# Expert stages' routing: router products within the norm, ranks by 16 wide products, one-hot tables in two operations, block experts behind them

## The reference, cut to what matters

```python
def _L0_ffn_ref(x):                       # 1024 tokens of 256, 2 experts, top 1
    probs = softmax(x @ gate_w.T); sel = argmax(probs)
    h = silu(x @ w_gate[e]) * (x @ w_up[e]); y = h @ w_down[e]
    return y[sel] * probs[sel]
def _L1_ffn_ref(x):                       # 8 experts, top 2
    probs = softmax(gelu(x @ rw1) @ rw2); wgt, idx = top_k(probs, 2)
    Ye = gelu(x @ w1[e] + b1[e]) @ w2[e] + b2[e]
    Ce = gelu(b1[e]) @ w2[e] + b2[e]      # for tokens that did not pick e
    return sum over e, k of active * wgt[k] * where(idx[k] == e, Ye, Ce)
x = x + 0.5 * L0_ffn(layernorm(x))
x = x + L0_attn(layernorm(x))
x = x + 0.5 * L0_ffn(layernorm(x))
x = x + 0.5 * L1_ffn(layernorm(x))
x = x + L1_attn(layernorm(x))             # a state-space mixer
x = x + 0.5 * L1_ffn(layernorm(x))
```

## Time and profile before

| | us |
|---|---|
| median of 3 runs | 1038.74 (1035.82 to 1044.8) |
| the profiled execution | 1029.2 |
| its span, first to last instruction | 1027.6 |
| PE busy | 860.1 (84%) |
| DVE, POOL, ACT busy | 595.2, 494.0, 396.2 |
| mean granted clock of PE | 0.939 |

### The profile page before, as it was taken

How to read it: one execution, slowest core, us unless ns; L and a number is a source line. 1 busy time by engine, 2 the same in 40 slices (tenths; PEclk the granted TensorE clock), 3 DMA queues, 4 the chain that set the end, 5 groups by cost and what they waited for, 6 DMA issues and landing times.

```text
span 1027.6 us, 21524 instructions
## 1 busy us (share of the span) xinstructions
PE 860.1 (84%) x7796; PEld 553.8 (54%) x7797; DVE 595.2 (58%) x1107; ACT 396.2 (39%) x955; POOL 494.0 (48%) x536
## 2 busy tenths in 40 slices
PE   3089986778778878999899999868789878999995
PEld 2046642323322334665589999433334444799994
DVE  5623346659888252334655565646589846556555
ACT  6322223127546442223245445356301224444441
POOL 2326758418888531212255453313688832555530
PEclk9999998989989989998799999889999998999997
DMA  8312655445555316202376664230000002666644
GB/s 295 111 39 91 204 181 158 168 179 182 179 180 160 109 46 277 110 16 73 107 249 222 246 228 146 93 138 1 0 1 0 1 6 103 230 245 232 234 160 139
DMA packets 47817, 142.25 MB, mean 138 GB/s; under 512 B 10641, under 2 KB 23778, under 8 KB 41218
## 3 DMA queue, kind: packets, MB, share of 16 engines
q0 software_dynamic: 19280, 93.40, 26.9%
q1 hardware_dynamic: 22430, 40.92, 11.3%
q10 hardware_dynamic: 6036, 6.95, 2.0%
HBM read 106.11 MB, written 35.16 MB: 137 GB/s over the span
## 4 chain that ended last, share of the span: by engine, by line
PE 64%; DVE 14%; DMA 8%; ACT 6%; issue 5%; SPq 2%; POOL 1%; ACTq 0%; DVEq 0%; POOLq 0%
PE psum L570 17%; PE psum L543 12%; PE psum L529 9%; PE psum L1831 4%; PE psum L1324 3%; PE psum L114 2%; DMA wq_dram<-mem 2%; PE psum L554 2%; DMA max_dram<-mem 2%; DVE mem L1454 2%; PE psum L1858 2%; PE psum L516 1%; PE psum L1296 1%; DVE mem L315 1%; PE psum L1272 1%
## 5 line engine op out<-in xcount | busy, mean ns | idle before, releaser
L570 PE MATMUL psum<-mem 128*128 x1536 | 178.9, 273 | 3.6 <-DVE mem L810 2.4
L570 PEld LDWEIGHTS psum<-mem 128*128 128x128 f16 x1536 | 146.3, 98 | 24.0 <-issue 4.8
L919 POOL DMA_INDIRECT y_dram<-mem x64 | 63.6, 993 | 155.2 <-DVE mem L826 153.3
L543 PE MATMUL psum<-mem 128*128 128x128 f16 x2208 | 130.8, 219 | 0.0
L543 PEld LDWEIGHTS psum<-mem 128*128 128x128 f16 x2208 | 126.8, 98 | 0.7
L661 ACT ACTIVATE mem<-psum,mem 128x128 f32<-128x128 f32 x368 | 105.0, 369 | 52.7 <-PE psum L543 51.2
L914 POOL DMA_INDIRECT mem<-xn_dram,mem x64 | 66.8, 1044 | 106.1 <-PE psum L516 79.0
L1408 ACT ACTIVATE mem<-psum 128x512 f32<-128x512 f32 (+1 forms) x160 | 79.9, 552 | 81.9 <-PE psum L1304 53.4
L114 PE MATMUL psum<-ones 128*128 128x512 f16 x324 | 102.5, 441 | 0.6 <-issue 0.6
L529 PE MATMUL psum<-mem 128*128 x432 | 99.7, 389 | 1.6 <-issue 1.6
L1454 DVE TENSOR_REDUCE mem<-psum 128x2 f32<-128x1024 f32 (+2 forms) x96 | 87.9, 948 | 22.3 <-PE psum L1278 12.7
(11 more groups left out here) (250 smaller groups left out, 1477.0 us busy)
## 6 DMA issues: line engine op xcount, KB each, us to landing
stage<-in_w POOLq DMA_DIRECT2D x20, 480.0 KB, 4.9
stage<-in_w POOLq DMA_DIRECT2D x16, 512.0 KB, 4.3
w_rows<-mem SPq DMA_DIRECT2D x8, 1024.0 KB, 7.6
w2h_dram<-mem POOLq DMA_DIRECT2D x20, 240.0 KB, 2.9
w2l_dram<-mem POOLq DMA_DIRECT2D x20, 240.0 KB, 3.4
xn_dram<-mem ACTq DMA_DIRECT2D x32, 128.0 KB, 1.7
mem<-w2h_dram SPq DMA_DIRECT2D x2, 2048.0 KB, 12.7
mem<-w2l_dram SPq DMA_DIRECT2D x2, 2048.0 KB, 17.9
```

Source lines behind the costliest of these rows:

```text
L543: ins = eng.matmul(c.bank(2 * p + j // half)[:, j % half * P:(j % half + 1) * P], mats[q][:, l, k, j * P:(j + 1) * P], x[:, p, k, :], star ...
L570: ins = eng.matmul(c.bank(6)[:, 0:D], a[:, 0 if gated else p, q * half + j, :], w[:, at], start=(i == 0), stop=(i == 3 * CF - 1))
L919: eng.indirect_dma_start(c.y_dram[:, :], bass.IndirectOffsetOnAxis(ap=yidx[:, b:b + 1], axis=0), yo[:, b % 2, :], None).then_inc(s_ys[b % ...
```

## The change

- `layernorm_stage` takes a function `between`, which PE calls for each tile behind its transposes, and a `table`, an activation function that ACT runs once on one element ahead of the norm. Gated: the router products of tiles 0 to 5 are issued in the norm (0, 1 and 2 with tile 4), those of tiles 6 and 7 behind it. Otherwise: the six products of half 0 are issued two by two with tiles 5, 6 and 7, each pair in place of two of the three idle products. The idle products in the norm behind attention write to bank 4 instead of 5.
- ACT runs one more element of Silu or Gelu behind the Exp (not in stage 1).
- Ranks: one product per choice of `before16` with the masks of all tiles (64 columns, 16 gated), then for each tile u and choice one product of `ones16` with u's masks, repeated for all tiles behind it. All accumulate in one region. 16 products instead of 72 (8 instead of 36 gated).
- `ends`, `ebc`, `ebf`, `widx`, `ebi` stand behind the one-hot tables in DVE's order. `ebc` compares with 7 (1) experts instead of 8 (2); two operations disappear (the product by P with the minimum, and a minimum).
- `pcol`, `sbase16`, `eqb` and the counting rows `iota16` are fp16, the latter copied from fp32 at the start of the program. The 16 (8) one-hot tables are made by two two-tensor operations of 8 (4) tables each.
- POOL makes `idb` first, then waits for `widx` and issues slab 0, rows 0, slab 1, rows 1, slab 2, rows 2 and so on, instead of slab 0, slab 1, `idb`, rows 0, rows 1, slab 2.

```diff
@@ -167,6 +167,8 @@
         return c.bank(6 + i % 2)[:, 0:D].rearrange("p (k t) -> p k t", k=KD)
     def act(eng):
+        if table is not None:
+            eng.activation(c.spent[:, 0:1], c.ln_consts[:, 0:1], table)
         for i in range(NT + 1):
             if i < NT:
                 t = order[i]
...
@@ -195,8 +197,9 @@
             for k in range(KD):
                 ins = eng.transpose(pst(i)[:, k, :], XN[:, order[i], k * P:(k + 1) * P], c.ident[:, :])
             ins.then_inc(s_tps.sem, 1)
+            worked = between(eng, i) if between is not None else 0
             if "idle_bank" in src:
-                keep_awake(c, eng, src["idle_bank"], 3)
+                keep_awake(c, eng, src["idle_bank"], 3 - min(worked, 2))
     return dict(dve=dve, act=act, pe=pe, pool=pool, xn=s_xn, hi=s_hi, lo=s_lo)
...
@@ -332,8 +335,50 @@
         eng.dma_start(c.xn_dram[1 + t * P:1 + (t + 1) * P, :], XN[:, t, :]).then_inc(s_xs.sem, 16)
-    L = layernorm_stage(c, src, XN, stored, W["bias_part"] is None)
     order = src["order"]
+
+    def router_tile(eng, n):
+
+        t = order[n]
+        eng.wait_ge(*L["lo"](n + 1))
+        tok = slice(t * P, (t + 1) * P)
+        i = 0
+        for k in range(KD):
+            for a, b in ((c.XTh, W["gh"]), (c.XTh, W["gl"]), (c.XTl, W["gh"])):
+                ins = eng.matmul(c.bank(5)[:, t * E:(t + 1) * E], a[:, k, tok], b[:, k, :],
+                                 start=(i == 0), stop=(i == 3 * KD - 1))
+                i += 1
+        return ins
+
+    ROUTER = [(k, a, b) for k in range(KD) for a, b in (("r1h", c.XTh), ("r1l", c.XTh), ("r1h", c.XTl))]
+
+    def router_half(eng, s, steps):
+
+        tok = slice(s * BANK, (s + 1) * BANK)
+        for i in steps:
+            k, a, b = ROUTER[i]
+            ins = eng.matmul(c.bank(s), W[a][:, k, :], b[:, k, tok], start=(i == 0), stop=(i == len(ROUTER) - 1))
+        return ins
+
+    def router_between(eng, i):
+
+        if i == 4:
+            for ready in W["router_ready"]:
+                eng.wait_ge(*ready)
+        if gated:
+            if i >= 4:
+                for n in ((0, 1, 2) if i == 4 else (i - 2,)):
+                    router_tile(eng, n)
+            return 0
+        if i < 5:
+            return 0
+        eng.wait_ge(*L["lo"](NT // 2))
+        ins = router_half(eng, 0, range(2 * (i - 5), 2 * (i - 4)))
+        if i == NT - 1:
+            ins.then_inc(s_hid.sem, 1)
+        return 2
+
+    L = layernorm_stage(c, src, XN, stored, W["bias_part"] is None, router_between, None if gated else ACT.Gelu)
     NE = NT * E
     KT = TOPK * NT
     lg = region.take([NT, E], F32)
...
@@ -346,15 +391,16 @@
     wk = region.take([TOPK, NT], F32)
     wkh = region.take([TOPK, NT], F32)
     slotf = region.take([TOPK, NT], F32)
-    pcol = region.take([TOPK, NT], F32)
+    pcol = region.take([TOPK, NT], F16)
     sbase = region.take([TOPK, NT], F32)
+    sbase16 = region.take([TOPK, NT], F16)
     full = region.take([NT, E], F32)
     t4 = region.take([TOPK, NT, E], F32)
     cmp8 = region.take([E, NT], F32)
     nblk = region.take([E], F32)
     before = region.take([E], F32)
     ends = region.take([E], F32)
-    ebc = region.take([NB, E], F32)
+    ebc = region.take([NB, E - 1], F32)
     ebf = region.take([NB], F32)
     ebi = region.take([NB], I32)
     idx = region.take([NB], U32)
...
@@ -439,29 +485,13 @@
                 W["bias_part"](eng, i)
                 keep_awake(c, eng, 3, 1)
         L["pe"](eng)
-        for ready in W["router_ready"]:
-            eng.wait_ge(*ready)
         if gated:
-            for n, t in enumerate(order):
-                eng.wait_ge(*L["lo"](n + 1))
-                tok = slice(t * P, (t + 1) * P)
-                i = 0
-                for k in range(KD):
-                    for a, b in ((c.XTh, W["gh"]), (c.XTh, W["gl"]), (c.XTl, W["gh"])):
-                        ins = eng.matmul(c.bank(5)[:, t * E:(t + 1) * E], a[:, k, tok], b[:, k, :],
-                                         start=(i == 0), stop=(i == 3 * KD - 1))
-                        i += 1
+            for n in range(NT - 2, NT):
+                ins = router_tile(eng, n)
             ins.then_inc(s_lg.sem, 1)
         else:
-            for s in range(HALVES):
-                eng.wait_ge(*L["lo"]((s + 1) * NT // HALVES))
-                tok = slice(s * BANK, (s + 1) * BANK)
-                i = 0
-                for k in range(KD):
-                    for a, b in ((W["r1h"], c.XTh), (W["r1l"], c.XTh), (W["r1h"], c.XTl)):
-                        ins = eng.matmul(c.bank(s), a[:, k, :], b[:, k, tok], start=(i == 0), stop=(i == 3 * KD - 1))
-                        i += 1
-                ins.then_inc(s_hid.sem, 1)
+            eng.wait_ge(*L["lo"](NT))
+            router_half(eng, 1, range(len(ROUTER))).then_inc(s_hid.sem, 1)
             for t in range(NT):
                 eng.wait_ge(*s_hida(t // (NT // HALVES) + 1))
                 ins = eng.matmul(c.bank(5)[:, t * E:(t + 1) * E], hid[:, t * P:(t + 1) * P], W["r2"],
...
@@ -482,11 +512,13 @@
                 ins = eng.matmul(out, c.ones16[:, :], mk[:, k, t, :], start=(i == 0), stop=(i == len(todo) - 1))
             if m == 0:
                 ins.then_inc(s_cn.sem, 1)
-        for t in range(NT):
-            out = c.bank(5)[:, NE + t * E:NE + (t + 1) * E]
-            todo = [(c.before16, k, t) for k in range(TOPK)] + [(c.ones16, k, u) for u in range(t) for k in range(TOPK)]
-            for i, (m, k, u) in enumerate(todo):
-                ins = eng.matmul(out, m[:, :], mk[:, k, u, :], start=(i == 0), stop=(i == len(todo) - 1))
+        ranks = c.bank(5)[:, NE:2 * NE].rearrange("p (t e) -> p t e", e=E)
+        for k in range(TOPK):
+            ins = eng.matmul(ranks, c.before16[:, :], mk[:, k, :, :], start=(k == 0), stop=False, skip_group_check=True)
+        for u in range(NT - 1):
+            for k in range(TOPK):
+                ins = eng.matmul(ranks[:, u + 1:NT, :], c.ones16[:, :], mk[:, k, u, :].unsqueeze(1).to_broadcast([P, NT - 1 - u, E]),
+                                 start=False, stop=(u == NT - 2 and k == TOPK - 1), skip_group_check=True)
         ins.then_inc(s_rk.sem, 1)
         if W["bias_part"] is not None:
...
@@ -497,7 +529,7 @@
             keep_awake(c, eng, 2, 6 if gated else 10)
         eng.wait_ge(*s_idb(1))
         for i in range(KT):
-            eng.wait_ge(*s_oh(i + 1))
+            eng.wait_ge(*s_oh(2 * i // KT + 1))
             ins = eng.matmul(c.bank(3)[:, 0:NB], oh[:, i, :], idb[:, i, :], start=(i == 0), stop=(i == KT - 1))
         ins.then_inc(s_ids.sem, 1)
...
@@ -640,6 +672,8 @@
                 eng.activation(hid[:, s * BANK:(s + 1) * BANK], c.bank(s), ACT.Gelu).then_inc(s_hida.sem, 1)
         eng.wait_ge(*s_d(1))
         eng.activation(ex[:, :, :], lg[:, :, :], ACT.Exp).then_inc(s_ex.sem, 1)
+        if weights_act is None:
+            eng.activation(c.spent[:, 1:2], c.ln_consts[:, 0:1], ACT.Silu if gated else ACT.Gelu)
         if weights_act is not None:
             weights_act(eng)
...
@@ -736,15 +770,6 @@
         link(eng.tensor_reduce(nblk[:, :], cmp8[:, :, :], AX.X, ALU.add))
         link(eng.tensor_tensor(cmp8[:, :, 0:E], c.tri128[:, 0:E, 0:E], nblk[:, :].unsqueeze(1).to_broadcast([P, E, E]), ALU.mult))
         link(eng.tensor_reduce(before[:, :], cmp8[:, :, 0:E], AX.X, ALU.add))
-        link(eng.scalar_tensor_tensor(ends[:, :], nblk[:, :], float(P), before[:, :], ALU.mult, ALU.add))
-        link(eng.tensor_tensor(ebc[:, :, :], c.iota_b[:, 0:NB].unsqueeze(2).to_broadcast([P, NB, E]),
-                               ends[:, :].unsqueeze(1).to_broadcast([P, NB, E]), ALU.is_ge))
-        link(eng.tensor_reduce(ebf[:, :], ebc[:, :, :], AX.X, ALU.add))
-        eng.tensor_scalar(ebi[:, :], ebf[:, :], float(E - 1), None, ALU.min).then_inc(s_eb.sem, 1)
-        if not gated:
-            link(eng.tensor_scalar(spare[:, :], ebf[:, :], float(E - 1), float(P), ALU.min, ALU.mult))
-            eng.tensor_scalar(widx[:, :], spare[:, :], c.row_spare[:, :], float(1 + TOP2 * T), ALU.add, ALU.subtract).then_inc(s_wi.sem, 1)
-            eng.wait_ge(*s_wi(1))
         eng.wait_ge(*s_rk(1))
         link(eng.scalar_tensor_tensor(full[:, :, :], c.bank(5)[:, NE:2 * NE].rearrange("p (t e) -> p t e", e=E), -(P - 1) / 2,
                                       before[:, :].unsqueeze(1).to_broadcast([P, NT, E]), ALU.add, ALU.add))
...
@@ -753,15 +778,24 @@
         link(ins)
         link(eng.tensor_reduce(slotf[:, :, :], t4[:, :, :, :], AX.X, ALU.add))
         link(eng.tensor_scalar(sbase[:, :, :], slotf[:, :, :], 1 / P, ROUND, ALU.mult, ALU.add))
-        link(eng.tensor_scalar(sbase[:, :, :], sbase[:, :, :], ROUND, float(P), ALU.subtract, ALU.mult))
-        link(eng.tensor_tensor(pcol[:, :, :], slotf[:, :, :], sbase[:, :, :], ALU.subtract))
-        eng.tensor_tensor(eqb[:, :, :], c.iota_b[:, 0:NB].unsqueeze(1).to_broadcast([P, KT, NB]),
```

(35 more changed lines are left out.)

14 lines of the change are left out of this document (8 added, 6 removed).

## The result

The changed kernel is slower by 0.65%: ratio to the kernel before **1.0065, 95% interval 1.0033 to 1.0097**, with medians of 1041.56 us against 1037.18 us (20 runs each). The ratio leaves out the runs more than 1.5% above the fastest of their kernel (7 of 20 before, 2 of 20 after). It stands for 6.7 us where the forecast had +0.3. Over all 20 runs the means differ by 4.1 us (95% interval 0.5 to 7.6) and the medians by 4.4, so the sign is firm and the size is not: 4 to 7 us by these figures. On the 1038.74 us of the forecast the ratio makes 1045.5, above the 1043 at which its range ended. Run again later beside other kernels the changed kernel gave 1.0061 [1.0022, 1.0100], and 1.0042 over all runs. Its profiled execution took 1035.28 us (span 1033.6).

What follows compares the result with a forecast made beforehand. PE work bounds the run (64% of the chain of waits), so only stretches ahead of expert blocks can gain. Terms -0.6 - 1.1 - 0.85 - 0.55 + 3.4 = +0.3 us make 1039.0 us for the median, range 1032 to 1043.

Steps and rivals of the forecast that it cites:

- Norm and router: PE's router ahead of the blocks: gain 0.8 us in stages 3 and 4 (eight experts), 0.5 in stage 2, 0 in stage 1.
- Ranks, ends and tables: DVE's routing chain, stages 3 and 4: ends off the front gain 1.5 us, ranks hidden, tables gain 1.1, 0.7 comes back.
- The 0.6 us of overlap: One-hot tables, stage 4: sixteen alone 3.5 of 4.10 us, the other 0.6 POOL's product, which both kernels have.
- Stages 1 and 2: The gated stages: stage 1 gains 0.6 us, passing whole to block 0, and stage 2 gains 1.1; together -1.7.
- Stages 3 and 4, slab 0's issue: POOL issues slab 0 (t0) 0.28 us behind widx; if the old 1.5 us delay returns, stage 3 is +0.4.
- Rows 1's landing: Stages 3 and 4: rows 1 lands at t0 + 8.9, block 0 starting 0.85 and 0.55 us sooner than before.
- The clock: PE stands 2 to 3 us between turns of rows 0 and 1; low clock costs 1.7 us each in stages 3 and 4.
- Rival C: Stages 3 and 4: 1.5 us slab delay in both, low clock costing 1 more each; +4.7 us, 1043.4; chance 0.13.
- Rival B: Stages 3 and 4: rows don't queue behind slabs, no long stand; -6.7 us with stages 1 and 2, 1032.0; chance 0.15.
- A: Stages 3 and 4: as the forecast, but the clock holds or falls where PE stands anyway; -3.1 us, 1035.6; chance 0.20.
- The prediction's own sign of error: The forecast is wrong if block 0 starts more than 2 us earlier in its stage, from the last XTl, than before.

Runs made afterwards that it cites:

- the move undone: Changed kernel with ends to widx again ahead of the ranks and slabs 0 and 1 issued there; ratio to the kernel before 0.9949, repeated 0.9945.
- The experiment with a third slab: The move undone, with slab 2 issued right behind POOL's product, ahead of the row gathers; ratio to the kernel before 1.0053.
- The experiment without idle products: The move undone, without the sixteen idle products ahead of turn 0 in stages 3 and 4; ratio to the kernel before 1.0008.
- the move alone: Kernel before with only ends to widx put behind the sixteen old table operations, and POOL's new order; ratio to the kernel before 1.0104.
- the old tables: The move undone, with the tables made again by sixteen (eight) old one-hot operations on f32 columns; ratio to the kernel before 0.9987.
- the gated stands filled: The move undone, idle products added: 34 between turns in stage 1, two behind stage 2's routing, two between turns in stages 2, 3, 4; ratio 0.9967.

## Why the prediction was wrong

**Norm and router: right.** The logits come 0.81 and 0.82 us sooner in stages 3 and 4 (0.8 forecast) and 0.6 in stage 2 (0.5).

**Ranks, ends and tables: right to 0.1 us.** The rank products end at 864.04 + 0.50, ahead of L774's start at 864.86. The two table operations take 2.96 us (3.0 forecast). Slab 0's issue in stage 4 comes 871.22 - 856.98 = 14.24 us behind the end of the last XTl; forecast 870.67 - 856.36 = 14.31. The 0.6 us of overlap that I took over from the old kernel came out, in part by luck: the old rows were misread. Their tables start 0.195 us apart, so sixteen alone take 3.2 us, and POOL's product cost the old kernel 0.9, not 0.6. It is the time in which DVE stands for the product, 0.6 to 0.7 us here. The Trainium skill ("SBUF — State Buffer", Who interferes with whom) says that a DVE tensor_tensor with both inputs in SBUF and a GpSimd operation that reads SBUF exclude each other for a whole instruction; the rows above agree, with 0.81 us against 1.48 and 1.72. This rule would have priced POOL's product right ahead of the run. That the old operations, with one tensor input, stand for the product too is known here from the rows alone. The product's length is off the path here, since the last table product waits for DVE.

**Stages 1 and 2: the start right, the pass-through wrong.** Turn 0 of stage 1 comes 0.7 us sooner (0.6 forecast). But turn 1 waits for attention's weight operations on DVE, whose own pace varies: in five executions with the same code up to there it came between 31.00 and 31.89, before 32.00. Over these five block 2 gains 0.35 us on average, where 0.6 was forecast. In stage 2 block 0 starts 1.09 us sooner (1.1 forecast), and then takes 7.99 us instead of 5.35, with block 1 at 5.34 instead of 6.41; 0.14 us is left at block 2. In all five executions with this code block 0 took 7.99 to 8.09 us there; with the move undone, which does not touch PE's program, it took 5.35 to 7.89. What decides between them no run shows. The forecast priced a low clock only in stages 3 and 4.

**Stages 3 and 4, slab 0's issue: right in one, wrong in the other.** Stage 4's is 0.28 us behind widx as forecast. In stage 3 the 1.5 us came back, as it does in the kernel before and with the move undone. The text had named it as +1.2 to that stage's sum; it should have been in the forecast, since both stages of the old trace showed their own delay and nothing in the change touched it.

**Rows 1's landing: the term that failed.** The step "rows 1 lands after two slabs and rows 0: t0 + 7.7 + 2 x 0.6 = t0 + 8.9" has the right mechanism and the wrong size. Turn 1 came at t0 + 10.5 in stage 3 and t0 + 11.3 in stage 4. Already rows 0, behind one slab, was turned at t0 + 6.1 and t0 + 7.0, not t0 + 5.8, and 4.4 us more followed for slab 1 and rows 1, not 3.1. Three things were short. The 7.7 us were read too early: 5.0 us at 382 GB/s are 1.9 MB, and two slabs hold 2.1, which had moved only at t0 + 8.2. Those slabs had the DMA engines to themselves, whereas here the stretch ran at 336 GB/s with short row packets between the slabs. And the sum had nothing for slab 2, and at most 0.25 us for the time from the last packet to PE. The windows show both together: the rate falls to 230 GB/s from 879.70 to 881.20, as rows do, and is back at 411 from 881.70 while PE still stands until 882.50; by then some 0.65 MB of slab 2 had moved (0.56 in stage 3: 10.48 us at 279 GB/s). How much of the wait is slab 2 sharing the engines, and how much is a completion that comes late, the rates don't separate. The experiment with a third slab gave 3.7 us for one slab (7.1 against 3.4 from issue to turn), where the sum had 2.5. Block 0 so started 2.1 us (stage 3) and 1.9 us (stage 4) later than before instead of 0.85 and 0.55 sooner. That is 5.4 us in the two stages, 1.2 of it stage 3's slab delay.

**The clock: right in kind, its sum right partly by luck.** PE stood 3.97 and 3.92 us between the turns (2 to 3 forecast), the clock was 0.51 over stage 4's stand and 0.50 in the last microsecond of stage 3's, and the distance from block 0 to block 2 grew by 2.2 us in stage 3 and 1.2 in stage 4: 3.4 in all, as forecast, though neither is the 1.7 of the sum and the stands were longer than it had. The experiment without idle products gave 1.2 to 1.9 a stage.

**Sum.** Forecast for the four stages: -0.6, -1.1, -0.85 + 1.7, -0.55 + 1.7 = +0.3. By the trace at block 2: -1.6 (-0.35 over five), -0.1, +4.4, +3.1 = +5.7 (+7.0), and by the timed runs 6.7 (4.1 over all 20). From +0.3 to +7.0 it is 4.3 us for rows 1's landing, 1.2 for slab 0's delay, 1.0 for stage 2's low clock and 0.2 for stage 1. Rival C, at +4.7, was the nearest case: it had the late slab, though in both stages where one had it, and a longer low clock, but not the longer queue. Rival B is excluded by the third slab. A was excluded by block 0's 4 to 5 us.

The prediction's own sign of error was a block 0 more than 2 us sooner in its stage. The error lay on the side it did not watch, 1.9 and 2.1 us later.

## What to carry to other kernels

Before moving a computation off the critical chain, look at what its result issues: here 1.5 us of DVE work was taken out of the chain, and with it two 1 MB transfers were moved from the time in which the DMA engines lay idle into the way of a small gather that everything waits for. Here it paid to issue the large transfer early or behind the small one, and not right ahead of it. Price a large transfer that lies ahead up to the moment at which the small one was used in a trace, not up to the end of the fast stretch at its best rate. Look at the second and the third use of the buffers too: letting only the first small gather pass moved the same wait one block on.

## What the runs showed of the hardware

- One slab (128 rows of 8 KB) issued 2.1 us ahead of a row gather on the same software queue, behind two others, moves the turn of the gather's rows in stage 4 from 4.3 to 7.1 us behind the issue, which stays where it was. Where no idle products stood ahead of the turn, it came at 3.4.
- POOL's 368-element product takes 0.81 us beside DVE operations of 0.27 us with one tensor input, and 1.48 to 1.72 beside operations of 1.22 us with two. DVE stands in both cases: its longest operation is 1.45 and 1.82 us long there.
- POOL's first slab gather goes out 1.5 us behind the end of widx in stage 3, in the kernel before (1.55), the changed one (1.54) and the ones with the move alone and with the move undone (1.55), with no releaser in the trace ("issue"), and 0.28 us behind it in stage 4. No run told why.
- In some executions the blocks pause. Between turns that are 5.5 to 5.7 us apart there were single gaps of 7.0 us in the changed kernel (7.6 in its repetition), 10.0 with the old tables and 9.7 in the kernel with the gated stands filled, with ACT's gelu waiting for something that the trace names only as remote. Timeline of the changed kernel:

```profile
951.11 1.14 ACT L695 ACTIVATE mem<-psum,mem 128x128 f32<-128x128 f32 x4 [3.33 <-remote]
```

The kernel before had none in its profiled execution. The kernel with the move undone had none in its first profile (span 1019.1 us) and three, of 8.1 to 8.7 us, in its second (1033.8), at the same code and the same timed ratio. So the pauses belong to an execution and not to an edit; they are part of the spread of 1% between runs, and one profile's span would have ranked these kernels wrongly. What causes them stays open.
